# A 16-head attention stage rewritten: query halves, projections for two heads through DRAM, shifted maxima

## The chip, the cores and the metric

The kernel runs on one core of one Trainium2 chip. The metric is device time in microseconds (us) of one execution. Three runs of the kernel before gave 2880.21, 2882.32 and 2882.97 us; the median is 2882.32.

## The reference

Two layers, each a cross attention and an expert layer. The change touches the first attention only:

```python
        x = layer_norm(x, ln_m_g, ln_m_b)
        lat = layer_norm(latents, ln_l_g, ln_l_b)
...
        q = lat @ Wq
        kv_input = jnp.concatenate([x, lat], axis=1)
        kv = kv_input @ Wkv
        k, v = jnp.split(kv, 2, axis=-1)
...
        dots = jnp.einsum('bhid,bhjd->bhij', q, k) * scale
        attn = jax.nn.softmax(dots, axis=-1)
        out = jnp.einsum('bhij,bhjd->bhid', attn, v)
        out = out.transpose(0, 2, 1, 3).reshape(b, m, heads * dim_head)
        return out @ Wout
```

There are 6404 context rows (`x` here) and 1024 latents, so 7428 keys, and 16 heads of 64. There are 1024 queries (the latents), D is 128, everything is float32.

## The kernel before

The stages run one after the other: `stage_prepare` (layer norms, transposes, weights split into a high and a low float16 part), `stage_attention`, `stage_attention_out`, experts, cross attention, experts. Every float32 factor is a high 16-bit part plus a low one, and products of both are added in PSUM, TensorE's accumulators.

In `stage_attention` each of the 16 heads has two passes over the 7428 keys, which are 58 tiles of 128 keys and a tail of 4.

- Maxima (L485 to L496): for 128 queries at a time, high parts only, TensorE scores 1024 keys (a "slot"), ScalarE copies them to bfloat16 (L672), VectorE folds them into a running maximum (L774). 56 slots and 4 rest steps make a head. The maximum of each query, moved by a constant, goes into the rows 64 to 127 of `qd` (L517, L659), so that the scores of the second pass come out with it subtracted.
- Attention (`attend`): for one key tile and all 1024 queries, TensorE forms the scores (L535: `kc` with `qc`, `kd` with `qd`, four matmuls of 512 columns), ScalarE takes the exponential (L678, 128x1024) into `prob`, VectorE subtracts the upper 16 bits from it into `prob_low` (L800), and TensorE multiplies with the values: the upper 16 bits of `prob` with the high part of v and a column of ones (L553, 65 columns) and with the low part of v (L554, 64 columns), eight times each, and `prob_low` with the high part (L565, 65 columns, eight times).

A tile step of `attend(h)` holds tile t of head h and one slot of the maxima of head h + 1, so four engines' programs are written by hand in one fixed order and meet by semaphores. Between two heads stands `project`: keys, queries and values of head h + 2 from the normalised rows (`kvh`, `kvl`) by L433 to L463, in PSUM banks that attention and maxima leave free, split by ScalarE and VectorE, in the order that `between_heads` lists. No tensor goes through DRAM, and the GpSimd engine (POOL) has no part in the attention but two fills at its start.

Of the kernel before, what the change touches and what calls it, by code (L numbers as in the profile page):

```python
# [11 lines left out]
F16 = mybir.dt.float16  # L12
BF16 = mybir.dt.bfloat16
ALU = mybir.AluOpType
# [17 lines left out]
KEY_COLS = KEY_TILES * P  # L32
# [3 lines left out]
V_GROUPS = -(-KEY_TILES // 8)  # L36
VCOLS = 2 * DH + 1
BODY = 14
BODIES = FULL_TILES // BODY
LOOP_TILES = BODY * BODIES  # L40
MAX_CHUNKS = 7
MAX_SLOTS = TOKEN_TILES * MAX_CHUNKS
REST_COL = MAX_CHUNKS * 2 * BANK
REST = KEYS - REST_COL
REST_STEPS = TOKEN_TILES // 2
# [111 lines left out]
def stage_prepare(nc, pers, A):  # L157

    sc = Scope(nc, "prep", pers.whole)
    with sc:  # L160
# [41 lines left out]
        def _(act):  # L202
# [6 lines left out]
            for n in range(CL):  # L209
                norm_sqrt(act, nk, n * PER, (n + 1) * PER, n + 1)  # L210
                if n == CL // 2:

                    act.wait_ge(w_in, 32)
                    for r in range(2):
                        act.activation(pers.wk_h[:, :, r, :], wkv[:, 0:INNER].rearrange("p (h d) -> p h d", d=DH), ACT.Copy)\
                           .then_inc(w_high, 1)
                        act.activation(pers.wq_h[:, :, r, :], wq[:, :].rearrange("p (h d) -> p h d", d=DH), ACT.Copy)\
                           .then_inc(w_high, 1)
                    act.activation(pers.wv_h[:, :], wkv[:, INNER:2 * INNER], ACT.Copy).then_inc(w_high, 1)
# [28 lines left out]
        def _(pool):  # L248
# [5 lines left out]
            pool.wait_ge(w_high, 5)  # L254
            for r in range(2):
                pool.tensor_tensor(pers.wk_l[:, :, r, :], wkv[:, 0:INNER].rearrange("p (h d) -> p h d", d=DH),
                                   pers.wk_h[:, :, r, :], op=ALU.subtract).then_inc(w_done, 1)
                pool.tensor_tensor(pers.wq_l[:, :, r, :], wq[:, :].rearrange("p (h d) -> p h d", d=DH),
                                   pers.wq_h[:, :, r, :], op=ALU.subtract).then_inc(w_done, 1)
# [67 lines left out]
def stage_attention(nc, pers, A):  # L327
# [4 lines left out]

    sc = Scope(nc, "att", pers.whole)
    with sc:
        kc = sc.sb("kc", [P, 2, KEY_COLS], F16)
        kd = sc.sb("kd", [P, 2, KEY_COLS], F16)
# [3 lines left out]
        prob = [sc.sb(f"prob{n}", [P, TOKENS]) for n in range(2)]  # L342
        prob_low = [sc.sb(f"prob_low{n}", [P, TOKENS], F16) for n in range(2)]
        scores16 = [sc.sb(f"scores16_{n}", [P, 2 * BANK], BF16) for n in range(2)]
        running = [sc.sb(f"running{n}", [P, 2 * BANK], BF16) for n in range(2)]
        loop_max = sc.sb("loop_max", [P, TOKEN_TILES])
# [1289 lines left out]
```

## Time and profile before

| | |
|---|---|
| median of three runs | 2882.32 us |
| the profiled execution: its span, first to last instruction | 2884.0 us |
| TensorE matmuls busy | 2658.8 us, 92% |
| VectorE busy | 2348.5 us, 81% |
| ScalarE busy | 2271.1 us, 79% |
| GpSimd busy | 55.4 us, 2% |
| mean granted TensorE clock | 0.957 of 2.4 GHz |

The span and the time of a run are the same to 2 us, so a change of the span can be read as a change of the time. Busy shares are means over very different stages: the attention stands between about 68 and 2498 us, and the rows below are taken from inside it. Matmuls overlap in the pipeline of TensorE: a row gives the start and the length of each until its result is out (0.19 or 0.38 us), while what one costs in a row of many is the distance of two starts.

### The profile page before, as it was taken

What the parts mean: (1) busy time and instruction counts of PE and PEld (TensorE: products, weight loads), DVE (VectorE), ACT (ScalarE), POOL (GpSimd) and SP (SyncE); (2) the same over time, 40 slices, a digit from 0 to 9 for tenths busy, and PEclk for the clock granted to TensorE, in tenths of its full rate; (3) what the DMA queues carried; (4) which work ended last, traced back from release to release, by engine and by line L of the source; (5) the groups of instructions that cost most, each with busy time, mean ns of one, the idle gap of its engine ahead of it and who ended that gap; (6) DMA issues with size and microseconds to landing.
All of it is one profiled execution on the core that took longest, in us unless ns stands there. A gap on an engine that the chain in (4) does not pass through costs nothing. (4 is left out here: it accounts for less than half of the span.)

```text
span 2884.0 us, 93692 instructions
## 1 busy us (share of the span) xinstructions
PE 2658.8 (92%) x35639; PEld 1734.1 (60%) x35639; DVE 2348.5 (81%) x3328; ACT 2271.1 (79%) x2645; POOL 55.4 (2%) x95
## 2 busy tenths in 40 slices
PE   2799999999999999999999999999999999959996
PEld 1256665656565656565656566666656566747884
DVE  8789897979797979798888888888979797547864
ACT  4889897979797979797979798988979795426652
POOL 2100000000000000000000000000000000012001
PEclk9999999999999999999999999999999999979998
DMA  2000000000000000000000000000000000060000
GB/s 75 1 2 1 2 1 2 1 2 1 2 1 1 1 1 1 1 2 1 2 1 2 1 2 0 2 1 2 1 2 0 2 1 2 8 169 1 2 2 10
DMA packets 16345, 22.30 MB, mean 8 GB/s; under 512 B 1960, under 2 KB 13808, under 8 KB 15728
## 3 DMA queue, kind: packets, MB, share of 16 engines
q1 hardware_dynamic: 12816, 14.55, 1.7%
q8 instruction: 212, 3.47, 0.5%
q10 hardware_dynamic: 3296, 4.10, 0.5%
q14 instruction: 21, 0.17, 0.0%
HBM read 18.13 MB, written 0.52 MB: 6 GB/s over the span
## 5 line engine op out<-in xcount | busy, mean ns | idle before, releaser
L800 DVE TENSOR_TENSOR att_prob_low<-att_prob 128x1024 f16<-128x1024 f32 (+1 forms) x944 | 1153.7, 1223 | 196.7 <-ACT att_prob L678 195.9
L678 ACT ACTIVATE att_prob<-all_banks 128x1024 f32<-128x1024 f32 (+1 forms) x944 | 966.0, 1025 | 112.8 <-PE all_banks L565 32.6
L672 ACT ACTIVATE att_scores<-all_banks 128x1024 bf16<-128x1024 f32 x768 | 783.2, 1024 | 0.9 <-PE all_banks L495 0.6
L553 PEld LDWEIGHTS all_banks<-att_v,att_prob 128*128 128x128 bf16 x7552 | 538.3, 99 | 117.5 <-issue 16.1
L553 PE MATMUL all_banks<-att_v,att_prob 128*128 (+1 forms) x7552 | 597.7, 193 | 5.1 <-ACT att_prob L678 5.1
L554 PE MATMUL all_banks<-att_v,att_prob 128*128 (+1 forms) x7552 | 598.5, 195 | 0.0
L554 PEld LDWEIGHTS all_banks<-att_v,att_prob 128*128 128x128 bf16 x7552 | 506.0, 98 | 101.6
L535 PE MATMUL all_banks<-att_qc,att_kc 128*128 (+1 forms) x1888 | 562.5, 379 | 0.0
L535 PE MATMUL all_banks<-att_qd,att_kd 128*128 (+1 forms) x1888 | 562.0, 379 | 0.0
L495 PE MATMUL all_banks<-att_kc,att_qc 128*128 (+1 forms) x1792 | 534.3, 380 | 19.0 <-ACT att_scores L672 14.2
L774 DVE TENSOR_TENSOR att_running<-att_running,att_scores 128x1024 bf16<-128x1024 bf16 x768 | 525.9, 685 | 13.9 <-ACT att_scores L672 13.5
L565 PEld LDWEIGHTS all_banks<-att_v,att_prob_low 128*128 128x128 f16 x7552 | 354.1, 98 | 227.0 <-DVE att_prob_low L800 31.1
L565 PE MATMUL all_banks<-att_v,att_prob_low 128*128 (+1 forms) x7552 | 386.9, 194 | 3.7 <-DVE att_prob_low L800 3.5
L535 PEld LDWEIGHTS all_banks<-att_qd,att_kd 128*128 (+1 forms) x1888 | 183.9, 97 | 224.6 <-issue 1.1
L633 ACT ACTIVATE att_kc<-all_banks 128x512 f32 (+2 forms) x240 | 138.2, 582 | 156.3 <-PE all_banks L435 150.0
L721 DVE TENSOR_TENSOR att_kd<-all_banks,att_kc 64x512 f32 (+2 forms) x240 | 155.0, 661 | 93.1 <-ACT att_kc L633 91.3
L495 PEld LDWEIGHTS all_banks<-att_kc,att_qc 128*128 (+1 forms) x1792 | 115.4, 97 | 50.1 <-ACT att_scores L672 32.9
L672 ACT ACTIVATE att_running<-all_banks 128x1024 bf16<-128x1024 f32 x128 | 131.1, 1024 | 10.7 <-PE all_banks L495 10.7
L535 PEld LDWEIGHTS all_banks<-att_qc,att_kc 128*128 (+1 forms) x1888 | 122.1, 98 | 8.2 <-issue 1.1
L449 PE MATMUL all_banks<-shared_wv_h,shared_kvh 128*128 (+2 forms) x944 | 99.9, 194 | 26.3 <-DVE att_v L732 15.0
L449 PEld LDWEIGHTS all_banks<-shared_wv_h,shared_kvh 128*128 128x128 f16 (+1 forms) x944 | 84.4, 98 | 57.3 <-DVE att_v L732 35.0
L649 ACT ACTIVATE att_v<-all_banks 128x512 f32 (+3 forms) x128 | 72.2, 564 | 46.7 <-PE all_banks L451 40.0
(276 smaller groups left out, 2810.3 us busy)
## 6 DMA issues: line engine op xcount, KB each, us to landing
prep_ctx<-in_ctx SPq DMA_DIRECT2D x5, 640.0 KB, 8.6
later_ctx<-in_ctx SPq DMA_DIRECT2D x1, 3200.0 KB
experts_up<-in_L_ffn_f SPq DMA_DIRECT2D x1, 2048.0 KB, 8.3
prep_wkv<-in_L_xattn_Wkv ACTq DMA_DIRECT2D x1, 1024.0 KB, 12.3
all_X<-in_x SPq DMA_DIRECT2D x1, 512.0 KB, 4.5
prep_wq<-in_L_xattn_Wq ACTq DMA_DIRECT2D x1, 512.0 KB, 14.5
wout_w<-in_L_xattn_Wout SPq DMA_DIRECT2D x1, 512.0 KB, 4.1
out<-all_X SPq DMA_DIRECT2D x2, 256.0 KB, 2.5
```

The source lines that it names most:

```text
L449: pe.matmul(o, th, wh, start=True, stop=False)
L495: last = pe.matmul(banks[:, i, :], lhs, rhs, start=True, stop=True)
L535: last = pe.matmul(st[:, i * BANK:(i + 1) * BANK], w, r, start=start, stop=not start)
L553: pe.matmul(O[:, j // 4, o:o + DH + 1], w, high, start=False, stop=False, skip_group_check=True)
L554: pe.matmul(O[:, j // 4, o:o + DH], w, low, start=False, stop=False, skip_group_check=True)
L565: last = pe.matmul(O[:, j // 4, o:o + DH + 1], w, high, start=False, stop=True, skip_group_check=True)
L633: act.activation(o, bank(n), ACT.Copy).then_inc(k_high, 1)
L672: act.activation(o[:, :], banks[:, :, :].rearrange("p a q -> p (a q)"), ACT.Copy).then_inc(max_copied, 1)
L678: act.activation(prob[t % 2][0:n, :], S[t % 2][0:n, :], ACT.Exp, scale=SCALE).then_inc(exp_done, 1)
L721: dve.tensor_tensor(o, bank(c)[0:DH, :], h, op=ALU.subtract).then_inc(k_split, 1)
L774: dve.tensor_tensor(r[:, :], r[:, :], scores16[c % 2][:, :], op=ALU.max).then_inc(max_taken, 1)
L800: dve.tensor_tensor(prob_low[t % 2][0:n, :], p, p.bitcast(BF16)[:, 1:2 * TOKENS:2], op=ALU.subtract)\
```

## The change

`stage_attention` is written anew for all engines; `stage_prepare` loses the doubled copies of the key and query weights.

- Work comes in units: a pair of key tiles with one half of the queries (512), 29 pairs and the tail, so 30 units for a half and 60 for a head. One exponential still covers 128x1024.
- The values' low part rides along: `prob`'s upper bits with 129 columns (high, ones, low) for three of the four query tiles of a half, with 65 and 64 for the fourth, because all must fit in the one PSUM bank `O`. `normalize_half` adds the two parts.
- The maxima take one 512-column chunk (`max_slot`, L572), two in each unit, and VectorE reduces it straight from PSUM (`take`, L805). ScalarE's bfloat16 copies and VectorE's running maxima are gone. `max_slot` of chunk n waits for `take` of chunk n - 2. The chunks are shifted by 24 units against the heads.
- Projections are made for two heads at once (128 columns of weights), one task in every third unit: 17 tasks for keys and queries during the even head of a pair, 15 for values during the odd one. They are staged, written to DRAM (`write_kq`, `write_v`), and loaded again by SyncE (`load_kq`, `load_v`) once a head.
- The subtraction into `prob_low` is GpSimd's in 44 of the 60 units (L531) and VectorE's in 16 (L818), those with g % 4 = 1 and the tail units.

```diff
-            pool.wait_ge(w_high, 5)
-            for r in range(2):
...
+            pool.wait_ge(w_high, 3)
...
+        def by_pool(g):
+            return g % 4 != 1 and g % SIDE != PAIRS
...
         @block.gpsimd
         def _(pool):
...
+            def head(b):
+                for g in range(UNITS):
+                    if by_pool(g):
+                        pool.wait_ge(exp_done, EXP0 + b * UNITS + g + 1)
+                        pool.wait_ge(low_done, LOW0 + b * UNITS + g - 2)
+                        p = prob[g % NP][:, :]
+                        pool.tensor_tensor(prob_low[g % NL][:, :], p, p.bitcast(BF16)[:, 1:4 * BANK:2],
+                                           op=ALU.subtract).then_inc(split_pool, 1)
...
+            def max_slot(m, e, n, turn):
...
+                pe.wait_ge(max_taken, 2 + m * SLOTS + n - 1)
+                pe.matmul(X[n % 2][:, 0:kwidth(c)], qc[:, e, j * P:(j + 1) * P],
+                          kc[:, e, c * BANK:c * BANK + kwidth(c)], start=True, stop=True).then_inc(max_scored, 1)
...
+            def head(b, e, with_max, projecting, i):
+                for g in range(UNITS):
+                    p = g % SIDE
+                    m, me, n = slots_at(b, e, g)
+                    slots = with_max or m is b
+                    if p:
+                        apply_high(b, e, g, i)
+                    if slots:
+                        max_slot(m, me, n, i if m is b else i + e)
+                    if p >= 2:
+                        apply_low(b, e, g - 2)
+                    side_task(b, e, g, with_max, projecting, i)
+                    if slots:
+                        max_slot(m, me, n + 1, i if m is b else i + e)
+                    next_score(b, e, g, with_max)
...
+            def take(m, n):
+                j, c = divmod(n, K_CHUNKS)
+                dve.wait_ge(max_scored, m * SLOTS + n + 1)
+                dve.tensor_reduce(part[:, j, c:c + 1], X[n % 2][:, 0:kwidth(c)], axis=AX.X, op=ALU.max)\
+                   .then_inc(max_taken, 1)
...
+            def head(b, e, with_max, projecting, i):
+                for g in range(UNITS):
+                    m, _, n = slots_at(b, e, g)
+                    slots = with_max or m is b
+                    if slots:
+                        take(m, n)
+                    t = task_at(e, g - 1) if projecting and g else None
+                    if t is not None:
+                        split_task(i + 1, t)
+                    if not by_pool(g):
+                        split(b, g)
+                    if slots:
+                        take(m, n + 1)
```

TensorE before, the rest of a tile step (after L553 and L554 in turns, eight times each) and the beginning of the next:

```order
L554 MATMUL all_banks<-att_v,att_prob 128x64
L490 REGISTER_ALU
L495 ISA
L495 MATMUL all_banks<-att_kc,att_qc 128x512
L495 ISA
L495 MATMUL all_banks<-att_kc,att_qc 128x512
L565 MATMUL all_banks<-att_v,att_prob_low 128x65 x8
L535 ISA
L535 MATMUL all_banks<-att_qc,att_kc 128x512 x2
L535 REGISTER_ALU
L535 MATMUL all_banks<-att_qd,att_kd 128x512 x2
```

TensorE after the change, one unit without a task (L572 is a chunk of the maxima, L628 `apply_low`, L596 and L597 the scores):

```order
L613 MATMUL all_banks<-att_v,att_prob 128x129 x3
L616 MATMUL all_banks<-att_v,att_prob 128x65
L618 MATMUL all_banks<-att_v,att_prob 128x64
L571 REGISTER_ALU
L572 MATMUL all_banks<-att_kc,att_qc 128x512
L411 REGISTER_ALU
L628 MATMUL all_banks<-att_v,att_prob_low 128x65 x8
L571 REGISTER_ALU
L572 MATMUL all_banks<-att_kc,att_qc 128x512
L596 MATMUL all_banks<-att_qc,att_kc 128x512
L597 MATMUL all_banks<-att_qd,att_kd 128x512
```

The columns of a unit are those of a tile step; the two chunks of maxima stand apart, each with a wait of its own, and eight of the 65- and 64-column matmuls have become part of six of 129.

VectorE before, two tile steps of `attend` (L800 is the subtraction, L774 the running maximum):

```order
L800 TENSOR_TENSOR att_prob_low<-att_prob 128x1024
L768 REGISTER_ALU
L773 REGISTER_ALU
L774 TENSOR_TENSOR att_running<-att_running,att_scores_0 128x1024
L798 REGISTER_ALU
L800 TENSOR_TENSOR att_prob_low<-att_prob 128x1024
```

VectorE after, around a unit with g % 4 = 1 (L805 is `take`, L782 the low part of a projection, L818 the subtraction):

```order
L804 REGISTER_ALU
L805 TENSOR_REDUCE att_part<-all_banks 128x1
L780 REGISTER_ALU
L782 TENSOR_TENSOR att_stage_l<-all_banks,att_stage_h 128x512
L814 REGISTER_ALU
L815 REGISTER_ALU
L818 TENSOR_TENSOR att_prob_low<-att_prob 128x1024
L804 REGISTER_ALU
L805 TENSOR_REDUCE att_part<-all_banks 128x1
```

The second `take` of the unit, on which TensorE's next chunk but one depends, stands behind the subtraction.

GpSimd before, from the weights' low parts to the end of the attention:

```order
L260 TENSOR_TENSOR shared_wv_l<-prep_wkv,shared_wv_h 128x1024
L160 UNCONDITIONAL_BRANCH
L411 UNCONDITIONAL_BRANCH
L414 MEMSET att_kd 64x15104
L416 MEMSET att_v 128x118
```

GpSimd after, inside the loop over heads; of four units in a row three stand here:

```order
L528 REGISTER_ALU
L531 TENSOR_TENSOR att_prob_low<-att_prob 128x1024
L528 REGISTER_ALU
L531 TENSOR_TENSOR att_prob_low<-att_prob 128x1024
L528 REGISTER_ALU
L529 REGISTER_ALU
L531 TENSOR_TENSOR att_prob_low<-att_prob 128x1024
```

The same subtraction as VectorE's L818 now runs on a second engine, for other units, at the same time.

## Rows read from the trace of the kernel before

**Rows 1.** The page, busy us (share of the span) and instructions
```profile
PE 2658.8 (92%) x35639; PEld 1734.1 (60%) x35639; DVE 2348.5 (81%) x3328; ACT 2271.1 (79%) x2645; POOL 55.4 (2%) x95
```

**Rows 2.** Windows (start:end, length, busy us of PE, PEld, DVE, ACT, POOL, clock)
```profile
304.15:454.43 150.28, 144.37 (x2022) 91.79 (x2020) 127.93 (x160) 128.91 (x143) 0.00 (x0) 0.97 0.01 2
2256.68:2393.55 136.87, 133.11 (x1980) 86.58 (x1978) 123.83 (x155) 123.60 (x134) 0.00 (x0) 0.99 0.00 1
2393.55:2497.52 103.97, 101.67 (x1672) 70.93 (x1672) 73.23 (x63) 61.45 (x60) 0.00 (x0) 0.96 0.00 1
68.60:174.10 105.50, 78.85 (x594) 31.71 (x595) 80.14 (x125) 83.43 (x111) 12.65 (x2) 0.92 0.00 1
```

**Rows 3.** Timeline of TensorE, one tile step (start, length, line, matmuls merged)
```profile
428.70 0.59 PE L535 MATMUL all_banks<-att_qc,att_kc 128*128 x2
429.13 0.59 PE L535 MATMUL all_banks<-att_qd,att_kd 128*128 x2
429.56 0.19 PE L553 MATMUL all_banks<-att_v,att_prob 128*128 x1
...
430.06 0.59 PE L495 MATMUL all_banks<-att_kc,att_qc 128*128 x2
430.49 0.41 PE L565 MATMUL all_banks<-att_v,att_prob_low 128*128 x8
430.73 0.59 PE L535 MATMUL all_banks<-att_qc,att_kc 128*128 x2
```

**Rows 4.** Timeline of ScalarE and VectorE, the same tile step and the head's end
```profile
429.84 1.02 ACT L678 ACTIVATE att_prob<-all_banks 128x1024 f32<-128x1024 f32 x1
...
434.68 0.69 DVE L788 TENSOR_REDUCE att_rest_max<-all_banks 128x2 f32<-128x520 f32 x1
435.28 1.21 DVE L800 TENSOR_TENSOR att_prob_low<-att_prob 128x1024 f16<-128x1024 f32 x1
436.42 0.69 DVE L788 TENSOR_REDUCE att_rest_max<-all_banks 128x2 f32<-128x520 f32 x1
```

**Rows 5.** Timeline of TensorE between two heads
```profile
440.70 0.61 PE L509 MATMUL all_banks<-att_kc,att_qc 128*128 x2 [3.73 <-issue]
...
442.49 0.63 PE L433 MATMUL all_banks<-shared_kvh,shared_wk_h 128*128 128x512 f16 x1
442.92 0.63 PE L434 MATMUL all_banks<-shared_kvl,shared_wk_h 128*128 128x512 f16 x1
```

**Rows 6.** Timeline of TensorE in the later cross attention, matmuls of 128 columns
```profile
2681.38 0.22 PE L1496 MATMUL all_banks<-cross_ctx_l,cross_pt_h 128*128 128x128 f16 x1
2681.43 0.22 PE L1497 MATMUL all_banks<-cross_ctx_h,cross_pt_l 128*128 128x128 f16 x1
2681.49 0.22 PE L1495 MATMUL all_banks<-cross_ctx_h,cross_pt_h 128*128 128x128 f16 x1
```

**Rows 7.** Timeline of GpSimd and VectorE in `stage_prepare`
```profile
35.24 2.11 POOL L258 TENSOR_TENSOR shared_wq_l<-prep_wq,shared_wq_h 128x1024 f16<-128x1024 f32 x1
37.32 2.12 POOL L260 TENSOR_TENSOR shared_wv_l<-prep_wkv,shared_wv_h 128x1024 f16<-128x1024 f32 x1
...
37.30 0.14 DVE L120 TENSOR_TENSOR prep_nk_b<-prep_nk_stats 4x1 f32<-4x1 f32 x1
37.37 2.08 DVE L121 TENSOR_TENSOR prep_nk_var<-prep_nk_stats 4x1 f32<-4x1 f32 x1
...
39.61 0.14 DVE L124 TENSOR_TENSOR prep_nk_b<-prep_nk_b 4x1 f32<-4x1 f32 x1
```

**Rows 8.** Timeline of ScalarE, GpSimd and VectorE in the cross attention
```profile
2606.17 0.62 ACT L1315 ACTIVATE cross_ctx_h<-later_ctx 128x512 f16<-128x512 f32 x1
...
2606.87 1.16 POOL L1291 TENSOR_TENSOR cross_ctx_l<-later_ctx,cross_ctx_h 128x512 f16<-128x512 f32 x1 [1.28 <-ACT cross_ctx_h L1315]
...
2606.96 0.69 DVE L1376 TENSOR_SCALAR_CACHE_REDUCE cross_scores<-all_banks 128x512 f32<-128x512 f32 x1
```

**Rows 9.** DMA issues of the page (KB each, median us to landing)
```profile
experts_up<-in_L_ffn_f SPq DMA_DIRECT2D x1, 2048.0 KB, 8.3
```

More of the change, by code:

```diff
@@ L341, in stage_attention @@
         qd = sc.sb("qd", [P, 2, TOKENS], F16)
[L342 to L346, printed above, removed]
-        rest_max = sc.sb("rest_max", [P, TOKEN_TILES])
+        NP, NL = 3, 3
+        prob = [sc.sb(f"prob{n}", [P, 2 * BANK]) for n in range(NP)]
@@ new lines, in apply_low @@
+            def apply_low(b, e, g):
+                wait_split(pe, b, g)
+                for i, t in tiles(g):
+                    for q in range(4):
+                        w = prob_low[g % NL][:, i * BANK + q * P:i * BANK + (q + 1) * P]
+                        o = q * VCOLS
+                        last = pe.matmul(O[:, o:o + DH + 1], w, v[:, e, t, 0:DH + 1], start=False, stop=True,
+                                         skip_group_check=True)
+                last.then_inc(low_done, 1)
@@ new lines, in head @@
+            def head(b, e, with_max, projecting, i):
+                for g in range(UNITS):
+                    if g + 1 < UNITS:
+                        exp(b, g + 1)
+                    elif with_max:
+                        exp(b + 1, 0)
+                    n = task_at(e, g) if projecting else None
+                    if n is not None:
+                        copy_task(i + 1, n)
+                    elif g == BACK_AT:
+                        place_top(b, e, 1)
+                    elif g == FRONT_AT and with_max:
+                        place_top(b + 1, 1 - e, 0)
@@ new lines, in head @@
+            def head(b, e, with_max, projecting, i):
+                for g in range(UNITS):
+                    m, _, n = slots_at(b, e, g)
[9 more added lines that the diff above has]
+                        take(m, n + 1)
+                        if n + 2 in (SLOTS // 2, SLOTS):
+                            finish_max(m, 0 if n + 2 < SLOTS else 1)
+                    if g % SIDE == PAIRS:
+                        normalize_half(b, g // SIDE)
@@ new lines, in _ @@
+            dve.memset(spare[:, 8:9], 0.0).then_inc(constants, 2)
+            for n in range(KQ_TASKS):
+                split_kq(0, n, pers.banks[:, n % 4, :], FIRST_H[n % NF], FIRST_L[n % NF])
+            for n in range(KQ_TASKS, TASKS):
+                split_v(0, n, pers.banks[:, n % 4, :])
+                for x in FIRST_SLOTS[n - KQ_TASKS]:
+                    take(0, x)
+                    if x + 1 == SLOTS // 2:
+                        finish_max(0, 0)
+            with dve.Fori(0, HEADS // 2 - 1) as it:
+                head(2 * it, 0, True, True, it)
+                head(2 * it + 1, 1, True, True, it)
```

822 lines of the change are left out of this document (385 added, 437 removed).

## The prediction

> **What bounds the kernel now.** I read the page first, then windows by head, then the timelines of one tile step and of the gap between two heads. By the page TensorE is busy for 92% of the span, VectorE 81%, ScalarE 79%, GpSimd 2% [rows 1]. The windows run from one head's normalisation to the next: a full head takes 150.2 us, the next to last 136.9, the last 104.0, and 105.5 pass from the attention's start to its first score (174.1 us) [rows 2]. The heads thus fill 174.1 to 2497.5, 2323.4 us. A tile step takes 2.03 us (428.70 to 430.73): scores 0.86, 16 matmuls of 64 or 65 columns 0.50 (31 ns each), maxima 0.43, `prob_low` 0.24 [rows 3]. 56 steps are 113.7 of the 150.2 us; about 36 go into the projections, the tail and the gap, where TensorE idles 3.73 us and then starts 512-column matmuls 0.43 apart, the 1.2 GHz level, against 0.215 in the tile step [rows 3, 5]. So TensorE is the bound in the steps and order and clock are between the heads.
>
> **The change, part by part.**
>
> *TensorE's own work.* A 128-column matmul costs 0.055 us [rows 6], so I take 0.056 for 129 columns. A unit is scores 0.86, six of 129 and four small ones 0.34 + 0.12 = 0.46, two chunks 0.43, eight small 0.245: 2.00 us. The merged matmul gives only 0.03. Of a head, 58 units without their maxima are 58 x 1.565 = 90.8, two tails 1.6, 7428 keys x 8 query tiles of maxima 24.9 (120 chunks, the 15th of a row being 260 columns). Tasks per pair of heads: 17 x 3 x 0.215 less the short chunk = 10.65, and 177 x 0.056 = 9.9 for values, 10.3 a head. The spreads and zero matmuls add 1.4. Sum 129.0 against 150.2: this alone is 21 us a head, since the stretch between heads and its low clock vanish. ScalarE falls to some 70 us a head (60 exponentials of 1.02 [rows 4] and nine copies).
>
> *VectorE.* A `take` reads 512 values from PSUM; the nearest row is L788, 520 of them, 0.60 from start to start [rows 4]. 120 of these, 16 subtractions of 1.14 and ten task parts of 0.6 to 0.7 are about 100 us of 129, not the bound in sum. But the second `take` of a unit with g % 4 = 1 stands behind the subtraction, and TensorE's chunk after the next waits for it.
>
> *GpSimd and the wait that I expect.* 44 subtractions of 2.08 to 2.12 us, by the same shape in `stage_prepare` (35.24, 37.32) [rows 7], are 92 us of 129: enough in sum. However, the same rows show that the two engines exclude each other: L121 on VectorE, 4 x 1 elements, normally 0.14 us, took 2.08 because it began 0.05 after GpSimd's 2.12 us instruction, and ended with it; L120, begun 0.02 before, took 0.14. Its inputs both lie in SBUF. The VectorE instruction that reads PSUM beside L1291 kept its 0.69 us [rows 8]. So `take` is free and the subtraction L818, both inputs in SBUF, is not.
>
> The Trainium skill, page "SBUF — State Buffer", section "Who interferes with whom", has this as a rule: a VectorE instruction with two SBUF inputs and a GpSimd instruction that reads SBUF share one read interface, which the first to start keeps for the whole instruction. By that rule, the trace agrees, and size does not matter; without it the unblocked sum below would stand.
>
> Which comes first? Count from the start of unit g (g % 4 = 1). ScalarE starts exp(g + 1) at 0.28 (429.56 to 429.84 [rows 3, 4]), ends at 1.30, and GpSimd starts 0.08 later (2606.79 to 2606.87 [rows 8]): 1.38. VectorE gets chunk n, started at 0.46 and out at 0.84, works 0.60 and is ready for L818 at 1.48, or 0.6 later if a task's low part stands between. GpSimd is first by 0.1 us. It holds until 3.50; L818 runs to 4.64; `take` ends at 5.33; TensorE's second chunk of unit g + 1 can start at 5.38. It would have been due at 2.00 + 0.46 + 0.215 + 0.245 = 2.92, or 3.56 where one of the two units has a task of 0.645. TensorE stands 2.46 or 1.82 us; behind it wait the scores of unit g + 3 and with them ScalarE. Seven such units of each kind are 30.0 us a head; g = 29 (a tail subtraction) 1.6; the end of the head and the normalisation's last multiply, two SBUF inputs again, 2 together. A head: 129.0 + 33.6 = 162.6.
>
> Bounds of the wait of L818: at least 0 (it arrives first), at most one GpSimd instruction, 2.12, or more if its bfloat16 operand of stride two is slower than the contiguous one of rows 7; I take the row.
>
> *DRAM detour.* A head's keys and queries are 3.25 MB and values 1.92 MB. The nearest row, 2048 KB in 8.3 us [rows 9], gives 12.8 and 7.6 us. Loads start two units before a head, and the third task of an even head must find its first buffer written at about 6 units: 16 us with the wait above, 13 without it; the write queued behind the loads lands near 17. In the first case I count 0, in the second 4 us for seven heads, 28. SyncE waits in order; none of its other waits is near.
>
> The page "SBUF — State Buffer", section "Door 1: The DMA port swizzle", says that 64 partitions reach only half of the ports, 218 GB/s; by it the first part would take 14.9 instead of 12.8 us, an estimate of two more microseconds. No run here shows it.
>
> *Start.* In `stage_prepare` two of five GpSimd subtractions go, and with them two waits of VectorE like L121: 4.5 us. Then 17 tasks at first at the low clock (13 x 1.28 + 4 x 0.65 = 19.2), writes 3, load 12.8, and 72 `take`s with 13 value tasks, 43 + 9 = 52: the first score at about 154, and 6 to 8 us of waiting for the first values and the first exponentials, 162 against 174.1. I take -12, bounds -25 and +5.
>
> *Sum.* 14 heads x 162.6 = 2276. Head 14 has no tasks: 118.7 + 14 x 2.46 + 3 = 156. The last: 24 units of 2.00 and 5 x 2.46 = 60.3, then 36 without maxima where GpSimd's three and VectorE's one exclude each other, (3 x 2.08 + 1.14) / 4 = 1.85 each, 66.6, and 1: 128. Together 2560, +237 on 2323.4. The later stages stay. 2884.0 + 237 - 12 = 3109 as a span, and runs lie 2 below the profiled span (2882.3 to 2884.0): **3107 us**, slower by 7.8%.
>
> **Rivals.**
>
> A. *VectorE wins the race* in units that have no task just before. 0.1 us decides, and each of the terms is good to a few hundredths. Then GpSimd waits 1.14, which it can afford, and L818 is done at 2.62, the chunk is released at 3.36: stall 0.45 or 0. Only g = 1, 13, 25, 37, 49, after a task, are late: 5 x 2.46. A head is 129.0 + 12.3 + 1 + 2 = 144.3; 14 of them 2020, then 127.5 and 118: 2266, -58. Span 2884 - 58 - 12 = 2814, run 2812. For it: exp could start earlier or later than in rows 4, since L742 has three waits. Against it: every term I have puts GpSimd first.
>
> B. *No blocking of consequence* between the long instructions. The stall after a task is then 3.97 - 2.92 = 1.05, five times, and 0.45 twice: 136.2 a head, 14 x 136.2 + 126.5 + 108 = 2141, -182; with the DRAM waits +28: 2884 - 182 - 12 + 28 = 2718. Against it stands L121 with 2.08.
>
> C. *The waits also lower TensorE's clock.* After its 3.73 us idle, matmuls ran at 1.2 GHz for ten microseconds, 5 lost [rows 5]. If one wait in three of the seven long ones did so, 2.3 x 5 = 12 us a head: 3107 + 16 x 12 = 3299. Against it: the waits are shorter, and the stretch from 68.6 to 174.1, busy 78.85 of 105.5 us, still had a mean clock of 0.92 [rows 2].
>
> D. *The change does not shorten TensorE's work*: a 129-column matmul might pay more than 0.056, say 0.062 as the pair did; then the unit stays at 2.03, +2 us a head, +32. It is inside the range.
>
> **How the numbers follow.** Forecast 0.57, A 0.20, B 0.12, C 0.08, anything else 0.03. Faster by more than 0.2% (what a measurement of this kernel can tell from no change) are A and B with a little of the rest: 0.33; the same 0.02; slower 0.65. The forecast's own range is 3000 to 3200: the wait of L818 from 1.6 to 2.5 us moves it by 15 x 0.5 x 14 = 105 each way. To leave out no more than 0.2 the range goes down to A and a little past it and to the foot of C: 2780 to 3215. B and most of C stay outside.
>
> **What would show it.** The step on TensorE: starts of 129-column L613 0.056 apart, 129 us of work a head. The lock: L818 with a mean of about 3.1 us instead of 1.22, beginning while L531 runs and ending 1.14 after it; every third L531, the one after L818's release, with about 3.2 instead of 2.1; `take` at 0.69 throughout. The stall: TensorE idle before L572, released by L805, 14 times a head, 1.8 to 2.5 us each. A head period of 162 to 163 us. A period near 144 with L818 at two sizes says A; L818 at 1.22 throughout and 136 says B; a clock row below 0.97 in the middle of heads says C. The forecast is wrong as a whole if L531 and L818 overlap.

## The result and the profile after

The changed kernel takes 3101.2 us, median of four runs (3096.26 to 3106.63), against 2882.64 us of the kernel before, four runs beside it: a ratio of 1.076, 95% interval 1.0746 to 1.0776. The forecast was 3107. The profiled execution has a span of 3104.8 us, against 2884.0.

The page after, the same row as [rows 1]:

```profile
PE 2546.0 (82%) x28121; PEld 1673.4 (54%) x28121; DVE 2292.1 (74%) x3540; ACT 1342.0 (43%) x1627; POOL 1513.6 (49%) x800
```

Every engine but GpSimd does less than before, and the kernel is longer: the time is in waits. Windows after, in the columns of [rows 2]: head 1, head 2, the two last heads, and the first 72 maxima before the first score.

```profile
340.64:497.47 156.83, 134.04 (x1600) 89.24 (x1598) 124.66 (x180) 69.56 (x77) 91.64 (x45) 0.99 0.21 59
497.47:667.25 169.78, 140.18 (x1502) 86.78 (x1503) 126.49 (x166) 72.67 (x80) 91.01 (x45) 0.96 0.21 60
2452.52:2602.69 150.17, 125.44 (x1437) 79.87 (x1436) 115.79 (x148) 61.72 (x62) 93.19 (x44) 0.99 0.08 23
2602.69:2720.61 117.92, 104.28 (x1345) 69.87 (x1343) 69.22 (x77) 59.09 (x59) 90.08 (x44) 1.00 0.01 2
104.90:174.90 70.00, 46.21 (x209) 20.43 (x210) 53.19 (x100) 8.36 (x15) 0.00 (x0) 0.70 0.18 60
```

Odd heads take 157, even ones from the second on 168 to 170. The forecast had one number, 162.6, for all. Now one unit with g % 4 = 1 and no task (it starts at 352.20) and the next, timelines of all engines (start, length, idle before and what ended it):

```profile
352.20 0.34 PE L613 MATMUL all_banks<-att_v,att_prob 128*128 128x129 f16 x3
352.35 1.43 DVE L805 TENSOR_REDUCE att_part<-all_banks 128x1 f32<-128x512 f32 x2
352.37 0.19 PE L616 MATMUL all_banks<-att_v,att_prob 128*128 128x65 f16 x1
...
352.48 1.02 ACT L742 ACTIVATE att_prob<-all_banks 128x1024 f32<-128x1024 f32 x1 [0.99 <-PE all_banks L597]
...
353.58 1.89 POOL L531 TENSOR_TENSOR att_prob_low<-att_prob 128x1024 f16<-128x1024 f32 x1 [2.79 <-ACT att_prob L742]
353.70 2.86 DVE L818 TENSOR_TENSOR att_prob_low<-att_prob 128x1024 f16<-128x1024 f32 x1
...
354.21 0.34 PE L613 MATMUL all_banks<-att_v,att_prob 128*128 128x129 f16 x3
...
355.67 2.64 POOL L531 TENSOR_TENSOR att_prob_low<-att_prob 128x1024 f16<-128x1024 f32 x1 [0.19 <-ACT att_prob L742]
...
356.48 1.87 DVE L805 TENSOR_REDUCE att_part<-all_banks 128x1 f32<-128x512 f32 x3
357.21 0.39 PE L572 MATMUL all_banks<-att_kc,att_qc 128*128 128x512 f16 x1 [1.25 <-DVE att_part L805]
```

GpSimd starts 1.38 after the unit's start, VectorE at 1.50. GpSimd is done at 355.47; VectorE ends at 356.56, 1.09 later, 2.86 after it began. Only then come the reductions, and TensorE's chunk. The same two instructions over the whole kernel (busy us, mean ns):

```profile
L531 POOL TENSOR_TENSOR att_prob_low<-att_prob 128x1024 f16<-128x1024 f32 x704 | 1461.0, 2078 | 1180.2 <-ACT att_prob L742 1125.7 <-PE all_banks L628 53.0
L818 DVE TENSOR_TENSOR att_prob_low<-att_prob 128x1024 f16<-128x1024 f32 x224 | 590.3, 2635 | 29.0 <-ACT att_prob L742 29.0
```

What TensorE waited for, by line (us, times, longest us):

```profile
PE all_banks L572 <- DVE att_part L805: 357.1, 251, 3.0
PE all_banks L572 <- issue: 77.3, 7, 21.8
```

The first row is the foreseen wait: 14 long ones (0.8 us and more) in each of the first 15 heads, six in the last, and short ones. The second row holds two things. Once it is 21.8 us before the first maxima, the wait for the first loads, for which the forecast had 16 (in e5 the same 21.8 us stand under the load of `qd`). Six times it is 8.9 to 9.5 us at the start of an even head, and this was in no part of the forecast. There the loop over pairs of heads jumps back, and SyncE has just started the loads for the next head. Timelines of TensorE and of SyncE's issues at the first such place:

```profile
489.90 0.45 SPq L462 DMA_DIRECT2D att_kc<-k_high  x1
...
495.91 0.53 PE L628 MATMUL all_banks<-att_v,att_prob_low 128*128 128x65 f16 x12
496.48 0.35 SPq L471 DMA_DIRECT2D att_v<-v_all  x1
505.81 0.60 PE L572 MATMUL all_banks<-att_kc,att_qc 128*128 128x512 f16 x1 [9.37 <-issue]
```

Before an odd head SyncE issues the loads of keys and queries in the same way (657.71 to 660.99 before head 3), but there is no jump, and the longest wait of TensorE there is 2.15 us, one of the 14.

### The profile page after: what moved, and what is told of

The parts are those of the page before. It is cut to its first block and busy times, and to the rows that moved or that the text cites. A ratio compares the mean times of both kernels' runs of the same rounds, so it can differ in the third digit from the quotient of the medians.

```text
span 3104.8 us, 74132 instructions
## 1 busy us (share of the span) xinstructions
PE 2546.0 (82%) x28121; PEld 1673.4 (54%) x28121; DVE 2292.1 (74%) x3540; ACT 1342.0 (43%) x1627; POOL 1513.6 (49%) x800
## 5 line engine op out<-in xcount | busy, mean ns | idle before, releaser
L531 POOL TENSOR_TENSOR att_prob_low<-att_prob 128x1024 f16<-128x1024 f32 x704 | 1461.0, 2078 | 1180.2 <-ACT att_prob L742 1125.7
L805 DVE TENSOR_REDUCE att_part<-all_banks 128x1 f32<-128x512 f32 (+1 forms) x1920 | 1228.2, 666 | 568.8 <-PE all_banks L572 557.2
L742 ACT ACTIVATE att_prob<-all_banks 128x1024 f32<-128x1024 f32 x960 | 968.1, 1009 | 1240.8 <-PE all_banks L597 1194.4
L572 PE MATMUL all_banks<-att_kc,att_qc 128*128 128x512 f16 (+1 forms) x1920 | 727.6, 383 | 434.9 <-DVE att_part L805 357.1
L597 PE MATMUL all_banks<-att_qd,att_kd 128*128 128x512 f16 (+1 forms) x1888 | 723.7, 383 | 0.0
L596 PE MATMUL all_banks<-att_qc,att_kc 128*128 128x512 f16 (+1 forms) x1888 | 723.1, 383 | 0.7 <-issue 0.7
L818 DVE TENSOR_TENSOR att_prob_low<-att_prob 128x1024 f16<-128x1024 f32 (+1 forms) x256 | 624.1, 2438 | 34.8 <-ACT att_prob L742 29.0
L613 PE MATMUL all_banks<-att_v,att_prob 128*128 128x129 f16 x5664 | 541.7, 222 | 3.6 <-ACT att_prob L742 3.6
L572 PEld LDWEIGHTS all_banks<-att_kc,att_qc 128*128 128x128 f16 x1920 | 189.1, 100 | 513.2 <-DVE att_part L805 418.9
L628 PEld LDWEIGHTS all_banks<-att_v,att_prob_low 128*128 128x128 f16 x7552 | 356.4, 98 | 115.6 <-issue 8.6
L628 PE MATMUL all_banks<-att_v,att_prob_low 128*128 128x65 f16 x7552 | 387.1, 195 | 3.0 <-POOL att_prob_low L531 1.9
L618 PE MATMUL all_banks<-att_v,att_prob 128*128 128x64 f16 x1888 | 372.5, 197 | 0.0
L597 PEld LDWEIGHTS all_banks<-att_qd,att_kd 128*128 128x128 f16 (+1 forms) x1888 | 185.3, 98 | 213.0 <-issue 8.2
L596 PEld LDWEIGHTS all_banks<-att_qc,att_kc 128*128 128x128 f16 (+1 forms) x1888 | 185.4, 98 | 133.4 <-issue 14.9
```

Source lines behind the costliest of these rows:

```text
L531: pool.tensor_tensor(prob_low[g % NL][:, :], p, p.bitcast(BF16)[:, 1:4 * BANK:2], op=ALU.subtract).then_inc(split_pool, 1)
L572: pe.matmul(X[n % 2][:, 0:kwidth(c)], qc[:, e, j * P:(j + 1) * P], kc[:, e, c * BANK:c * BANK + kwidth(c)], start=True, stop=True).then_in ...
L596: pe.matmul(o, kc[:, e, t * P:t * P + n], qc[:, e, q], start=True, stop=False)
L597: last = pe.matmul(o, kd[:, e, t * P:t * P + n], qd[:, e, q], start=False, stop=True)
L613: pe.matmul(O[:, o:o + VCOLS], w, v[:, e, t, :], start=False, stop=False, skip_group_check=True)
L618: last = pe.matmul(O[:, o:o + DH], w, v[:, e, t, DH + 1:VCOLS], start=False, stop=False, skip_group_check=True)
```

## The experiments

Twelve kernels were run, with the kernel before beside them (2880.78 to 2882.22 us).

**e1: all full subtractions on GpSimd**

```diff
-            return g % 4 != 1 and g % SIDE != PAIRS
+            return g % SIDE != PAIRS
```

> All 58 full subtractions of a head on GpSimd, VectorE keeps the two tails (4 keys). Theory (the two engines exclude each other while both read SBUF): the 14 waits of TensorE per head before L572, 2.09 us in a unit without a task and 1.42 with one, 24 us a head, go, since VectorE has no long instruction left with two SBUF inputs. GpSimd needs 1.89 + 0.04 us of each 2.01 us unit, so it just keeps up; in the last 36 units, which take 1.57 us without maxima, it is the bound (+13 us). Head period 132 to 134 for odd heads, about 145 for even ones (the 9.4 us at the loop's edge stay). 3104.8 - 14 x 24.2 - 27 + 1 = about 2740 us. Rival (GpSimd's reading costs TensorE or ScalarE something, or GpSimd at 94% of the unit falls behind): L531 gets longer than 1.95 and the run stays above 2850.

Measured 2719.1 us, ratio 0.9436 (0.942 to 0.9451). Head 1 and head 2, windows in the columns above:

```profile
319.59:451.15 131.56, 130.43 (x1600) 87.42 (x1598) 90.64 (x165) 69.63 (x77) 110.72 (x59) 1.00 0.25 70
451.15:595.17 144.02, 135.87 (x1502) 85.73 (x1503) 90.96 (x151) 72.75 (x80) 110.68 (x59) 0.96 0.24 68
```

L531 has a mean of 1.91 us. With no long wait left, TensorE's work of a head is 131.6 us; the difference to 156.8, 25.2, is what the waits cost, with a little lost to the clock behind them (rival C below). The last head takes 112.6 us; by my +13 for its last 36 units it would have been 119.

**e2: VectorE's subtraction one unit earlier**

```diff
-                    if not by_pool(g):
+                    if g % 4 == 0 and not by_pool(g + 1) and (g + 1) % SIDE != PAIRS:
+                        split(b, g + 1)
+                    if g % SIDE == PAIRS:
                         split(b, g)
```

> The same 16 subtractions of a head stay on VectorE, at the same place between the two takes, but of unit g + 1 instead of g, for g % 4 = 0. GpSimd is idle then, from 1.27 us after the start of such a unit until 1.38 us into the next. Lock theory: VectorE's L818 starts at 1.49, 0.2 us after GpSimd's L531 ended, and takes 1.2 us; the take behind it ends near 3.2 where TensorE wants its chunk at 2.92, so a wait of 0.3 (up to 0.9 beside a task) is left of 2.09 and 1.42: head period 136 to 139 for odd heads, total 3104.8 - 15 x 20 = about 2800 us. Rival (the wait comes from the place of the subtraction in front of the second take, not from GpSimd): nothing changes, 3100 us, because the place is the same.

Measured 2781.5 us, ratio 0.9654 (0.9638 to 0.967), odd heads 136.6. Both engines do the same instructions as in the changed kernel. Timelines of GpSimd and VectorE around one of them:

```profile
348.58 3.82 POOL L531 TENSOR_TENSOR att_prob_low<-att_prob 128x1024 f16<-128x1024 f32 x2 [0.86 <-ACT att_prob L742]
...
352.62 1.22 DVE L818 TENSOR_TENSOR att_prob_low<-att_prob 128x1024 f16<-128x1024 f32 x1
353.75 0.68 DVE L805 TENSOR_REDUCE att_part<-all_banks 128x1 f32<-128x512 f32 x1
...
355.19 1.89 POOL L531 TENSOR_TENSOR att_prob_low<-att_prob 128x1024 f16<-128x1024 f32 x1 [2.79 <-ACT att_prob L742]
```

VectorE starts 0.22 us after GpSimd's two ended (352.40) and needs its usual 1.22; so do 217 of the 224 subtractions of this run. The rival, that the place in front of the second `take` costs the time, would have kept 3100: it falls.

**e3: loads later**

```diff
-                            sp.wait_ge(scored, b * UNITS)
+                            sp.wait_ge(scored, b * UNITS + 5)
```

> SyncE starts the loads of keys, queries and values (5 MB) five units into a head instead of two units before it. Six times, at the jump back of the loop over pairs of heads, TensorE stands 9.4 us and then works 2 us at 1.2 GHz; before the change the gap at such a jump was 3.73 us, with no transfer beside it. Theory (the fetch of the instructions behind the jump queues behind these loads): the gap falls to about 4 us, even heads from 169.7 to 163, total 3101 - 6 x 6 = 3065 us. Rival (the gap is the cost of the jump in a longer body): 9.4 stays, 3101.

By its wait the edit starts the loads three units into a head, five later than before. Measured 3230.1 us, ratio 1.1205 (1.1186 to 1.1224): slower than both, and still half right. The gap at the jump fell to 3.5 to 3.8 us (second row, timeline of TensorE). What I overlooked is behind the loads in the queue (first row, ScalarE):

```profile
368.80 0.60 ACT L714 ACTIVATE att_stage_v<-all_banks 128x512 f16<-128x512 f32 x1 [11.11 <-DMA v_all<-att_stage_v]
...
857.25 0.60 PE L572 MATMUL all_banks<-att_kc,att_qc 128*128 128x512 f16 x1 [3.57 <-issue]
```

In the first row ScalarE stands 11.11 us: the small writes of staged projections now stand behind the loads; ScalarE's next copy needs the staging buffer, and the exponentials stand behind the copy. TensorE waited 7.3 to 13.0 us once a head.

**e4: nearly all on VectorE**

```diff
-            return g % 4 != 1 and g % SIDE != PAIRS
+            return g % 30 == 28
```

> GpSimd keeps 2 subtractions of a head (units 28 and 58), VectorE has the other 58. Lock theory: L818 takes 1.2 us everywhere. VectorE has 120 takes at 0.60, 58 x 1.08 and tasks of 6.5 to 10: about 145 us, more than TensorE's 132; head period 145 to 148, even ones 155 to 158, total 3104.8 - 15 x 11 = about 2940 us: giving GpSimd work cost more than it took off VectorE. Rival (GpSimd's help is worth what its busy time says, and the waits have another cause): the head gets longer than 157, over 3100.

Measured 3046.4 us, ratio 1.0581 (1.0563 to 1.0599). VectorE is busy 151.7 of a head's 154.0 us, so it is the bound; my 145 had 1.08 us for a subtraction, and the 56 of this head last 1.27 each and hold up the next instruction for 1.19, over 6 us more. Still 55 us faster than with GpSimd's help for 44 of 60 subtractions.

**e5: e1 with the loads spread**

```diff
-                    if g == 0 and b + 1 < HEADS:
-                        if b:
-                            sp.wait_ge(scored, b * UNITS)
...
-                        load_kq(b + 1)
+                    if g in (2, 8, 14) and b + 1 < HEADS:
+                        sp.wait_ge(scored, b * UNITS + g + 1)
...
+                        load_kq(b + 1, (g // 6 * 2, g // 6 * 2 + 1))
+                    if g == LAST - 8 and not e and b + 1 < HEADS:
+                        sp.wait_ge(scored, b * UNITS + g)
+                        load_v(b + 1)
```

> e1 (all full subtractions on GpSimd) with the loads of a head's keys and queries issued two at a time in units 2, 8 and 14 of the head before, and the values in unit 51, so that no load stands beside the loop's edge and no staging write stands behind more than two of them. Theory: the fetch at the edge waits behind loads, and e3 lost only because its loads delayed the writes that ScalarE's copies wait for. The gap at the edge falls from 9.1 to 3.6 us, six times, the wait of 5.6 us in the first head goes too, and no new wait comes up: 2719 - 33 - 6 = 2680 us. Rival (any load inside a head delays ScalarE's copies, as in e3, 7 to 12 us a head): 2719 + 16 x 8 = 2850.

Measured 2668.45 us, ratio 0.9267 (0.9251 to 0.9282): the fastest of all, 7.3% below the kernel before. TensorE's waits at the jump, and an odd and an even head:

```profile
PE all_banks L570 <- issue: 19.9, 6, 3.4
```

```profile
309.31:440.55 131.24, 130.17 (x1600) 87.44 (x1597) 90.58 (x166) 69.94 (x78) 110.74 (x59) 1.00 0.25 71
440.55:577.54 136.99, 134.78 (x1502) 84.86 (x1503) 90.91 (x152) 72.44 (x80) 110.68 (x59) 0.99 0.26 71
```

3.3 us each instead of 9.1, and no new wait. Since TensorE's clock also stays up better behind the shorter gap (0.99 against 0.96), an even head gains 7.0.

**e6: e5 without the 129-column matmuls**

```diff
-                            pe.matmul(O[:, o:o + VCOLS], w, v[:, e, t, :], start=False, stop=False,
-                                      skip_group_check=True)
-                            continue
+                            pe.matmul(O[:, o:o + DH + 1], w, v[:, e, t, 0:DH + 1], start=False, stop=False,
+                                      skip_group_check=True)
+                            pe.matmul(O[:, o + DH + 1:o + VCOLS], w, v[:, e, t, DH + 1:VCOLS], start=False,
+                                      stop=False, skip_group_check=True)
+                            continue
```

> e5 with the 129-column matmuls undone: 65 and 64 columns for all four query tiles. By the prediction's own term a pair of 65 and 64 takes 0.062 and one of 129 takes 0.056, six pairs a unit, 58 units a head: 2.1 us a head, e5 + 33 = 2713 us. Rival (a 129-column matmul costs as much as the pair): e5 within 5 us.

Measured 2703.5 us against 2668.45 of e5, 35 us; an odd head takes 132.98 instead of 131.24, an even one 139.96 instead of 136.99. So the merge is worth about 2 us a head, as worked out, a little less in an odd head and more in an even one.

**e7: a one-input instruction on VectorE**

```diff
-                dve.tensor_tensor(prob_low[g % NL][0:n, 0:w], p,
-                                  prob[g % NP][0:n, :].bitcast(BF16)[:, 1:2 * w:2], op=ALU.subtract)\
+                dve.tensor_scalar(prob_low[g % NL][0:n, 0:w], p, 0.001, None, ALU.mult)\
```

> The kernel after the change with VectorE's 16 subtractions a head replaced by a multiplication with a constant, which reads only the float32 values (one input in SBUF); it leaves out the subtraction of the high part there. Theory in its narrow form (VectorE is shut out only where it reads two operands from SBUF): L818 starts 1.49 after the unit's start as before and takes no longer than without GpSimd, 0.6 to 1.2 us; the waits of TensorE go down to 0.5 or less, head 133 to 136, about 2750 us. Rival (any read or write of SBUF by VectorE waits for GpSimd): L818 still ends only after L531, 1.8 us late, about 3050 us.

One run, 2972.8 us, odd heads 149.0. The rival's sign is there, an end behind L531, but not its time, by the timelines of GpSimd and VectorE:

```profile
354.77 1.89 POOL L531 TENSOR_TENSOR att_prob_low<-att_prob 128x1024 f16<-128x1024 f32 x1 [2.02 <-ACT att_prob L742]
...
354.88 2.33 DVE L818 TENSOR_SCALAR att_prob_low<-att_prob 128x1024 f16<-128x1024 f32 x1
```

VectorE's instruction is shut out until 356.66 though it has one input, and then needs only 0.55 us for 1024 columns, half of the 1.1 us of the subtraction; I call that double rate. So "two inputs" is too narrow.

**e8: GpSimd fills instead of subtracting**

```diff
-                        pool.tensor_tensor(prob_low[g % NL][:, :], p, p.bitcast(BF16)[:, 1:4 * BANK:2],
-                                           op=ALU.subtract).then_inc(split_pool, 1)
+                        pool.tensor_tensor(prob_low[g % NL][:, 0:1], p[:, 0:1], p[:, 1:2],
+                                           op=ALU.subtract)
+                        pool.memset(prob_low[g % NL][:, 1:2 * BANK], 0.0).then_inc(split_pool, 1)
```

> The kernel after the change with GpSimd's 44 subtractions a head replaced by one of a single column and a fill of the other 1023 with zero, which reads nothing from SBUF; the low parts of these units are left out. Theory (GpSimd shuts VectorE out by its reading): L818 keeps 1.2 us even where it lies beside a fill, TensorE's waits are 0.3 to 0.9 instead of 2.09 and 1.42, head 136 to 139, about 2780 us. Rival (any GpSimd instruction that touches SBUF does it): L818 ends 1.1 after the fill beside it.

One run, 2778.6 us, odd heads 136.5. Groups by shape (busy us, mean ns):

```profile
L533 POOL MEMSET att_prob_low<- 128x1023 f16 x704 | 669.7, 951 | 0.0
L819 DVE TENSOR_TENSOR att_prob_low<-att_prob 128x1024 f16<-128x1024 f32 x224 | 272.2, 1215 | 34.5 <-ACT att_prob L743 34.5
```

The single column comes first and puts the fill off by 0.13 us, so in most units VectorE is now ahead of the fill by 0.02 us, and these units prove little. But behind a task and in the two heads without tasks the fill is first, as in these timelines of GpSimd and VectorE, and VectorE is not held there either:

```profile
2301.08 0.95 POOL L533 MEMSET att_prob_low<- 128x1023 f16 x1
...
2301.14 1.22 DVE L819 TENSOR_TENSOR att_prob_low<-att_prob 128x1024 f16<-128x1024 f32 x1
```

Held until the fill's end it would have needed 2.0. GpSimd shuts VectorE out by a subtraction, which reads SBUF, and not by a fill, which only writes there.

**e9: a one-input copy from strided bfloat16**

```diff
-                dve.tensor_tensor(prob_low[g % NL][0:n, 0:w], p,
-                                  prob[g % NP][0:n, :].bitcast(BF16)[:, 1:2 * w:2], op=ALU.subtract)\
+                dve.tensor_copy(prob_low[g % NL][0:n, 0:w], prob[g % NP][0:n, :].bitcast(BF16)[:, 1:2 * w:2])\
```

> The kernel after the change with VectorE's 16 subtractions a head replaced by a copy of the upper 16 bits (bfloat16 with a stride of two, one SBUF input) into prob_low; it leaves out the subtraction there. In e7 the one-input instruction on float32 still ended only after GpSimd's, and then took 0.56 us for 1024 columns, double rate. Theory (VectorE is shut out where it uses a second way into SBUF, by a second operand or by its double rate): this copy runs at single rate, about 1.1 us, and is not shut out: it lies beside L531 with a mean of 1.1 to 1.3, head period 136 to 138 us, about 2785 us. Rival (any VectorE instruction that reads SBUF is shut out): it ends after L531, mean above 2.2, head near 150 to 156 us, above 2950.

One run, 2975.0 us, odd heads 149.0, L818 with a mean of 2.09. By its headline numbers this is the rival's case, but it does not decide: this copy too needed 0.55 us after GpSimd's end, so it ran at double rate, and my premise of a single rate was wrong.

**e10: ScalarE 0.03 us later**

```diff
                 act.wait_ge(scored, b * UNITS + g + 1)
+                if g % 4 == 2:
+                    act.activation(warm[:, :], zeros[0:1, 0:1], ACT.Exp)
```

> Nothing is taken away: in front of the exponential of the units with g % 4 = 2, and behind its wait for the scores, ScalarE does one more exponential of a single element, about 0.2 us. GpSimd's L531, which starts 0.08 after that exponential, then starts near 1.6 after the unit's start, VectorE's L818 at 1.49. Lock theory: VectorE now wins the race in the units that have no task just before, runs 1.2 us, GpSimd waits 1.0 and can afford it; TensorE's wait goes from 2.09 to 0.3 (or from 1.42 to 0) there; behind a task's low part GpSimd is still first. That is rival A of the prediction: five long waits a head instead of 14, head period 142 to 146 for odd heads, total 3104.8 - 15 x 13 = about 2910 us, faster although ScalarE does more. Rival (the order of the two starts doesn't matter): 3100 us or a little more.

Measured 3063.2 us, ratio 1.0634 (1.0616 to 1.0652), against the 2910 expected: the edit did not do what it was meant to. The extra instruction slipped in ahead of the next one, whose start moved from 0.28 to 0.31, and GpSimd was still first in 13 of 14 units. In the last one of a head (g = 57) VectorE was now first by 0.02 us: it needed 1.22 instead of 2.86, and TensorE's wait there went from 2.15 to 0.50. That is half of what a head gained (153.7 instead of 156.8); the other half is a stretch at 1.2 GHz that every odd head of the changed kernel has and head 1 here has not (rival C below).

**e11: one input at single rate**

```diff
-                dve.tensor_tensor(prob_low[g % NL][0:n, 0:w], p,
-                                  prob[g % NP][0:n, :].bitcast(BF16)[:, 1:2 * w:2], op=ALU.subtract)\
-                   .then_inc(split_dve, 1)
+                dve.tensor_reduce(prob_low[g % NL][0:n, 0:w // 2], p.rearrange("p (c two) -> p c two", two=2),
+                                  axis=AX.X, op=ALU.max).then_inc(split_dve, 1)
...
+            dve.memset(prob_low[1][:, :], 0.0)
```

> The kernel after the change with VectorE's 16 subtractions a head replaced by a maximum over pairs of the float32 values, 1024 columns read and 512 written (one SBUF input); it leaves out the subtraction there. Both one-input instructions so far, on float32 and on strided bfloat16, needed 0.55 us after GpSimd had ended, double rate; so e9 didn't test what it was meant to. This one should run at single rate, 1024 / 0.55 x 0.55 x 2 = about 1.1 us. Theory (VectorE is shut out where it uses a second way into SBUF, by a second operand or by double rate): it starts at 1.49 and ends near 2.6, beside L531, mean 1.1 to 1.3, head 136 to 138, about 2785 us. Rival (any VectorE read of SBUF is shut out): mean above 2.4, head 155, above 3050.

One run, 2803.9 us, odd heads 137.7. Timelines of GpSimd and VectorE:

```profile
344.85 1.90 POOL L531 TENSOR_TENSOR att_prob_low<-att_prob 128x1024 f16<-128x1024 f32 x1 [2.01 <-ACT att_prob L742]
...
344.96 1.21 DVE L818 TENSOR_REDUCE att_prob_low<-att_prob 128x512 f16<-128x1024 f32 x1
```

Started 0.11 after GpSimd, as L818 was in nine of 14 units, it runs beside it and ends 0.58 us before it; all 224 of them take 1.21 or 1.22. The Trainium skill, page "SBUF — State Buffer", section "Who interferes with whom", says just this: a VectorE instruction in a mode that uses two ports contends with GpSimd, one with two SBUF inputs contends with GpSimd's reads only, and a `tensor_reduce` on this chip never contends. The runs agree on all four, if the double rate is such a mode: 2.64 us (two inputs) and 2.09 (double rate) beside GpSimd's reading, 1.21 (one input, single rate), and 1.22 for two inputs beside a fill.

**e12: ScalarE 0.3 us later**

```diff
+        junk = sc.sb("junk", [P, 256])
...
                 act.wait_ge(scored, b * UNITS + g + 1)
+                if g % 4 == 2:
+                    act.activation(junk[:, :], zeros[:, 0:256], ACT.Exp)
```

> e10 with a larger extra exponential, 256 columns instead of one, since in e10 it cost the next one only 0.03 us and GpSimd was still first (1.39 against 1.49). Here the exponential of units with g % 4 = 2 should start near 0.55 instead of 0.28 after the unit's start, and GpSimd be ready near 1.65, VectorE at 1.49. Lock theory: VectorE wins except behind a task's low part (g = 1, 13, 25, 37, 49): nine of 14 long waits of a head shrink from 2.09 or 1.42 to 0.3 or 0; head about 146 instead of 156.8, run 2930 to 2960 us, with ScalarE doing 6 us more a head. Rival (order doesn't matter): above 3090 us.

Measured 2888.6 us, ratio 1.0024 (1.0014 to 1.0033), odd heads 141.0 to 142.7, better than the 146 and 2930 to 2960 expected. ScalarE has 240 instructions of 0.42 us more to do, 100 us in sum, nothing is taken away, and the kernel is 213 us faster than the changed one. In head 1 ten of the 14 subtractions now take 1.22 (224 in the run: 152 under 1.35 us, 3 before); of the long waits of TensorE four are left. Timelines of ScalarE, VectorE and GpSimd around one such subtraction (its line is L821 here, GpSimd's L532):

```profile
353.64 1.01 ACT L745 ACTIVATE att_prob<-all_banks 128x1024 f32<-128x1024 f32 x1
...
354.61 1.22 DVE L821 TENSOR_TENSOR att_prob_low<-att_prob 128x1024 f16<-128x1024 f32 x1
...
354.73 6.56 POOL L532 TENSOR_TENSOR att_prob_low<-att_prob 128x1024 f16<-128x1024 f32 x3 [2.03 <-ACT att_prob L745]
```

VectorE is first by 0.12 us and keeps its 1.22. GpSimd's three take 6.56 instead of 3 x 1.89 = 5.67: it waited, and TensorE did not notice.

## Why the prediction was right

*TensorE's own work.* Right within 2%: three matmuls of 129 columns take 0.17 us (352.20 to 352.37), 0.057 each; a unit between waits is 2.01 against 2.00. A head without waits takes 131.2 to 131.6 (e5, e1) against 129.0. The merge (twelve matmuls of 65 and 64 columns became six of 129, not eight, as the section on the change has it) was worked out at 2.1 us a head and brought 35 / 16 = 2.2 (e6). ScalarE came out at 70, VectorE at 125 a head, and at 105 where nothing holds it (e2), against 100.

*The race.* Right to two hundredths: 1.38 against 1.48 foreseen, 1.38 against 1.50 measured. e12 shows that this tenth of a microsecond decides.

*The wait.* The mechanism was right in each link; its size was too high. GpSimd's instruction takes 1.89, not the 2.08 to 2.12 of [rows 7]; L818 is done 1.09, not 1.14 after it; `take` starts 0.08 before L818's end, since two neighbours on VectorE overlap. So the chunk comes at 5.01 after the unit's start (357.21 - 352.20) instead of 5.38. It was due at 354.68 + 0.215 + 0.245 + 0.67 for the task = 355.81: a wait of 1.40, of which 1.25 is idle in the row. By unit lengths the waits are 1.42 beside a task and 2.09 without, against 1.82 and 2.46. Waits of a head: 25.2 against 33.6, so odd heads take 157.0. The 25.2 is a difference of two heads; the rows bear it out: in head 1 the 14 idle times add up to 21.8 us, the results that still come out before each (0.15 us in the row above) to 2.1, and a stretch at 1.2 GHz (rival C) to 1.6, together 25.5.

*The detour through DRAM.* Counted at 0 for the data, and from head 1 on no copy or matmul inside the heads waits long for them; in head 0 ScalarE stands 7.0 us once (until 200.94) for the write of a staging buffer, and TensorE behind it 3.6 us, the wait that e3 then had in every head. But its loads meet TensorE at the loop's edge. The step that failed is the sentence that the stretch between heads vanishes with its low clock: [rows 5] had shown 3.73 us of idle at the jump, and I ascribed it to what stood there. It stayed 3.3 to 3.8 us where no load was near (e3, e5) and was 8.9 to 9.5 beside the loads. Even heads therefore take 168.8 on average, 11.8 above odd ones, six times: the gap, and matmuls at the 1.2 GHz level behind it.

*Start.* Wrong in sign: first score at 174.9, not 162. The projections took 18.8 us (64.4 to 83.2) against 19.2, but the load was there only at 104.9, 21.8 us after them, not 16: 4.3 until it was issued instead of 3, and 17.4 for itself instead of 12.8 (the row that it was scaled from was one load of 2048 KB). And the 72 `take`s with their tasks lasted 70.0 us, not 52, since TensorE's mean clock was 0.70, more than half of the time at 1.2 GHz, and `take`, value matmuls and copies follow each other instead of overlapping. Here are one task's low part and six `take`s, timeline of VectorE:

```profile
130.47 0.76 DVE L790 TENSOR_TENSOR att_stage_v<-all_banks,att_stage_v 128x256 f16<-128x256 f32 x2 [1.20 <-ACT att_stage_v L714]
131.14 3.61 DVE L805 TENSOR_REDUCE att_part<-all_banks 128x1 f32<-128x512 f32 x6
```

VectorE had idled 1.20 us for ScalarE's copy before the low part; such a group lasts 5.8 us (70.0 / 12), of which the six `take`s are 3.6.

*The last heads.* 150.2 and 117.9 against 156 and 128. In the 36 units without maxima the two engines do exclude each other, but nearly all units take 1.57, TensorE's own time, and not 1.85. With GpSimd's real 1.89 the two need only 1.62 a unit (from 2690.18 on, twelve subtractions of GpSimd with VectorE's among them, for 16 units, last 25.86 us). No `take` stands behind VectorE here, and the little that is missing goes into the three buffers of `prob_low`. Before that the waits were 2.01 instead of 2.46 each, and the last head had six of them, not five.

*The sum.* Against the forecast: odd heads 7 x -5.6 = -39, even ones 6 x +6.2 = +37, head 0 +3, the two last -16, together -15 (2545.7 against 2560); start +13; later stages -2. That is 3104.8 for 3109. The total is better than its parts, and its nearness of 6 us is luck. By mechanism the two errors are larger than this list shows, because each even head holds both: the waits and the work of the 13 heads after the first were 5.6 us a head too high, 73 us, and the edge of the loop, 71 us, was left out.

*The rivals.* The ratio excludes A and B for this kernel, but their heads could be built. A was priced at 144.3 a head; e12, where VectorE wins except after a task, has 141.0 to 142.7. B was 136.2; e2 and e11, where nothing is blocked, have 136.6 and 137.7. Their totals, 2812 and 2718, were too low (e12 2888.6, e2 2781.5), because the loop's edge (71) and the start (13) are missing from them too; B's has 28 us of waits for DRAM besides, which did not come. C happened, but small. In every head from 1 to 14 of the changed kernel, odd or even, there are one or two short stretches at 1.2 GHz away from the jump, such as this one, behind the wait of 1.92 us that ends at 378.01 (windows, the columns of [rows 2]):

```profile
378.80:382.20 3.40, 3.40 (x33) 2.69 (x31) 1.04 (x2) 1.02 (x1) 1.04 (x2) 0.50 0.00 0
```

In e1 and e5, where the waits are gone, no head from head 1 on has one away from the jump, until the end of the last. What one costs is seen where heads with and without it alternate: 155.3 against 153.7 (e10) and 142.7 against 141.0 (e12), 1.6 to 1.7 us, and not 12 a head. D is refuted by e6.

*What was to be seen.* As said: L818 ends 1.09 after L531, `take` at 0.684, 14 long waits of TensorE before L572 per head, released by L805. Off: L818's mean is 2.64, not 3.1, from the shorter GpSimd instruction and because behind a task it starts later and takes 1.9 to 2.3; the L531 after it is 2.64, not 3.2, because it is shorter and starts 0.2 us after VectorE was let in. A clock of 0.96 in even heads comes from the gap at the jump: e1 has it too, without the waits.

## What to carry to other kernels

Work moved to an idle engine is free only if the two do not need the same way into memory: look for each pair of long instructions that can overlap, find out which starts first to a tenth of a microsecond, and who stands behind the loser. If there is such a pair, give all of that work to one engine or start it in the other's gap (e1, e2), before buying capacity. And ask of every burst of loads what else is fetched at that moment: the small writes behind it (e3), or perhaps the instructions behind a jump (e5).

## What the runs showed of the hardware

- VectorE instructions with one SBUF input are also held by GpSimd's reading when they run at double rate: 0.55 us of work for 1024 columns became 2.33 (e7, e9). At single rate they are not (1.21, e11). GpSimd's fills do not hold a VectorE subtraction (e8).
- A bfloat16 copy with a stride of two ran at double rate (e9), which I had not expected.
- The jump back of a loop cost TensorE 3.3 to 3.8 us of idle alone (e3, e5) and 8.9 to 9.5 beside some 5 MB of loads; 3.25 MB of loads without a jump cost it nothing that the rows show. That what waits there is the fetch of the instructions fits both moves of the loads, but is not shown: the profile names it only "issue".
- In the heads with long waits TensorE's clock fell to 1.2 GHz once or twice a head also away from the jump, and each time it cost 1.6 to 1.7 us (e10, e12).
- GpSimd's subtraction takes 1.89 us with a bfloat16 operand of stride two, less than the 2.12 us with a contiguous float16 one [rows 7].
